# Order of a carry matmul and two scans within the step of a graph attention phase

## What is computed

```python
# layer 0, attention with 8 heads of 16 channels; src, tgt per edge
hi = x[src] @ w1
hj = x[tgt] @ w2
e = leaky_relu(hi + hj, 0.3) * a
logits = e.reshape(-1, 8, 16).sum(-1)
exp = jnp.exp(logits - segment_max(logits, tgt)[tgt])
attn = exp / segment_sum(exp, tgt)[tgt]
x = layernorm(x + segment_sum(hi.reshape(-1, 8, 16) * attn[:, :, None], tgt))
# layer 1, messages from nodes and edge attributes
ef = (relu(attr @ We1 + be1) @ We2 + be2) * sigmoid(t @ Wt + bt)
msg = relu(concat([x[src], ef]) @ Wn1 + bn1) @ Wn2 + bn2
x = layernorm(x + segment_sum(msg, dst) + x)
```

## Time and profile before

| | before |
|---|---|
| median of three runs | 2203.7 us |
| lowest and highest | 2195.6 and 2203.87 us |
| the profiled execution's own time | 2198.74 us |
| span of the profile | 2196.7 us |
| busy: PE, PE weight loads, DVE, ACT, POOL | 81%, 63%, 60%, 30%, 73% |
| mean granted PE clock | 0.906 of full speed |

### The profile page before, as it was taken

The page is one execution under the profiler, slowest core; times in us unless marked ns, Lnnn a source line. Parts: engine busy times, 40 slices in busy tenths (PEclk is TensorE's granted clock), DMA queues, the critical chain, the costliest instruction groups (busy, mean ns, idle before and its releaser), DMA issues.

```text
span 2196.7 us, 47111 instructions
## 1 busy us (share of the span) xinstructions
PE 1779.1 (81%) x12650; PEld 1394.1 (63%) x12721; DVE 1325.3 (60%) x3725; ACT 659.2 (30%) x1410; POOL 1602.8 (73%) x1701
## 2 busy tenths in 40 slices
PE   6787777777888888877869888888888788888877
PEld 5465555655666666655657667666666676667666
DVE  6555666666556666656645456666566566665655
ACT  6111111121111111111114434434444344444432
POOL 5777777777777777777527777777777777777775
PEclk9889998999888888899879999989999999999998
DMA  8722333333333333333255444444444444454441
GB/s 238 153 78 85 84 95 84 96 97 91 89 94 86 96 97 87 91 90 96 56 142 154 139 126 139 129 135 135 141 127 131 137 132 137 128 142 127 141 125 46
DMA packets 239385, 252.30 MB, mean 115 GB/s; under 512 B 141011, under 2 KB 187720, under 8 KB 239315
## 3 DMA queue, kind: packets, MB, share of 16 engines
q1 hardware_dynamic: 185036, 141.15, 21.8%
q0 software_dynamic: 54000, 110.28, 19.4%
q10 hardware_dynamic: 288, 0.13, 0.0%
HBM read 233.20 MB, written 13.22 MB: 112 GB/s over the span
## 4 chain that ended last, share of the span: by engine, by line
POOL 54%; issue 23%; PE 11%; DVE 5%; DMA 4%; DVEq 1%; POOLq 1%; ACT 1%; SPq 0%; ACTq 0%
POOL T L741 32%; POOL G L707 21%; PE ps L1854 2%; DMA G<-hi_rows,idx 2%; PE ps L1831 2%; PE ps L1826 2%; PE ps L1858 1%; PE ps L1787 1%; DVEq L1316 1%; DVE msg L1336 1%; ACT V L895 0%; DMA T<-y_rows,idx 0%; PE ps L2060 0%; DMA out<-T 0%; PE ps L2069 0%
## 5 line engine op out<-in xcount | busy, mean ns | idle before, releaser
L741 POOL DMA_INDIRECT T<-y_rows,idx x831 | 788.1, 948 | 307.3 <-issue 251.8
L707 POOL DMA_INDIRECT G<-hi_rows,idx x831 | 799.7, 962 | 263.2 <-issue 249.5
L2060 PE MATMUL ps<-G 128*128 128x64 f32 x1664 | 223.0, 279 | 125.9 <-DVE acc L1613 125.0
L999 ACT ACTIVATE G<-G 128x512 f32<-128x512 f32 x208 | 131.1, 630 | 577.6 <-DVE G L1619 577.6
L2060 PEld LDWEIGHTS ps<-G 128*128 128x128 f32 x1664 | 211.9, 199 | 137.8 <-issue 137.2
L1826 PE MATMUL ps<-ident,G 128*128 128x128 f32 x828 | 147.9, 307 | 180.0 <-issue 92.8
L1619 DVE TENSOR_TENSOR G<-ps,T 128x512 f32<-128x512 f32 x208 | 143.6, 690 | 218.8 <-DMA T<-y_rows,idx 207.4
L2069 PE MATMUL ps<-wN,G 128*128 128x128 f32 x1664 | 254.2, 300 | 23.2 <-DVE T L1578 23.2
L895 ACT ACTIVATE V<-ps 128x512 f32<-128x512 f32 x207 | 123.7, 598 | 468.3 <-PE ps L1831 462.6
L1307 DVE TENSOR_TENSOR V<-ps,V 128x512 f32<-128x512 f32 x207 | 141.8, 685 | 184.5 <-ACT V L895 181.9
L2081 PEld LDWEIGHTS ps<-msg,wE 128*128 128x128 f32 x832 | 170.2, 205 | 127.2 <-issue 112.3
(11 more groups left out here) (238 smaller groups left out, 2238.7 us busy)
## 6 DMA issues: line engine op xcount, KB each, us to landing
T<-in_edge_weight SPq DMA_DIRECT2D x103, 512.0 KB
Dbc<-block_destinations SPq DMA_DIRECT2D x69, 384.0 KB
T<-in_edge_attr SPq DMA_DIRECT2D x103, 256.0 KB
G<-hi_rows,idx POOLq DMA_INDIRECT x831
T<-y_rows,idx POOLq DMA_INDIRECT x831
link<-scan_destinations SPq DMA_DIRECT2D x280, 16.1 KB
hi_rows<-T SPq DMA_DIRECT2D x12, 256.0 KB, 4.6
mX<-in_x SPq DMA_DIRECT2D x15, 192.0 KB
```

Source lines behind the costliest of these rows:

```text
L707: pool.indirect_dma_start(out=G[:, s, t * C:(t + 1) * C], out_offset=None, in_=hi_d[:, :], in_offset=bass.IndirectOffsetOnAxis(ap=idx[:, s ...
L741: pool.indirect_dma_start(out=Yb[:, r, t * C:(t + 1) * C], out_offset=None, in_=y_d[:, :], in_offset=bass.IndirectOffsetOnAxis(ap=idx[:, r ...
L2060: ins = pe.matmul(sums_of(g4), hS[i][:, n * C:(n + 1) * C], ohB[i][:, n * W:(n + 1) * W], start=(n == 0), stop=(n == 3))
```

## The change

Two groups of statements change places with a neighbour, in the step of the first phase. On PE the downward carry, with its waits, stands ahead of aggregate(0); on DVE the second and third scan, with theirs, ahead of add(0).

```diff
@@ DVE, in step
                     leaky(2)
-                    add(0)
                     if b is not None:
 
                         dve.wait_ge(s_sh1, b + 1)
...
                         dve.tensor_tensor_scan(R3[0:BR, ::-1], link[:, bs, P:0:-1], R2[0:BR, ::-1], -1e30, ALU.add,
                                                ALU.max).then_inc(s_r3, 1)
+                    add(0)
                     nxt(2)
                     add(1)
@@ PE, in step
                     sums(2)
-                    aggregate(0)
                     if b is not None:
                         pe.wait_ge(s_r1, b + 1)
 
                         need(pe, s_msg, b)
                         pe.matmul(shp[0:BR, 0:1], down[0:BR, 0:BR], R1[0:BR, P - 1:P], start=True, stop=True).then_inc(s_sh1, 1)
+                    aggregate(0)
                     logits(f, s, 1)
```

## The result

| | before | after |
|---|---|---|
| median of 10 runs each | 2199.17 us (2194.6 to 2203.87) | 2205.24 us (2198.93 to 2209.6) |
| ratio after to before | | 1.0024, 95% interval 1.0013 to 1.0035 |
| profiled execution | 2198.74 us, span 2196.7 | 2205.65 us, span 2203.6 |

The change costs about 5 us, a quarter of a per cent.

A forecast was written before the change was run, and what follows sets the result against it. The prediction took POOL's issue of gathers to bound the first phase, with PE, DVE and ACT fitting beneath. Terms 0 + 0 + 4 + 0 + 0 = +4 us on 2198.7 gave 2203; it took 2204, range 2194 to 2216.

The forecast's parts named there:

- The wait on the first scan: First phase, PE: the carry matmul's new wait, 30 to 68 us in all, absorbed by PE's room; 0 on the path.
- Second and third scan earlier: First phase, DVE: scans start sooner but nothing takes their results sooner; gain on the path 0, at most 1.2 us.
- Collisions: First phase: delayed window one-hots lengthen POOL's gathers that start inside them; +4 us, bounds -9 to +21 us.
- The drain: Between the two phases' gathers: the carry matmul only changes places with aggregate(0); 0 us, 3 us allowed either way.
- Rival B: First phase: the new wait makes PE and DVE the bound, using up the message margin; about 2218 us, chance 0.05.
- the 2229 us: Whole kernel: total if the 30 us of new PE waits were paid in full; no chance of its own.
- Rival C: First phase: window one-hots settle just ahead of a gather in 30 steps now just clear; +21 us, 2220, chance 0.09.

The follow-up runs named there:

- iota_before: The kernel before, with the window one-hots' counting columns read from a PSUM bank instead of SBUF; ratio 0.9953 to before, 2192.34 us.
- iota_after: The changed kernel with the window one-hots' counting columns read from PSUM instead of SBUF; ratio 0.9955 to before, 2192.16 us.
- after_third: The changed kernel run again unaltered, on another chip beside 17 runs of the kernel before; ratio 1.0026 to before.
- dve_only: The kernel before with only DVE's half: second and third scan ahead of add(0), PE in the old order; ratio 1.0007 to before.
- pe_only: The kernel before with only PE's half: downward carry ahead of aggregate(0), DVE in the old order; ratio 0.9994 to before.

## Why the prediction was right, point by point

The forecast was no change within half a per cent, at 2204 us, with the cost, if any, in the gathers; measured 2205.24. That the time came within 1.3 us is partly luck. The forecast's change of +4 us started from a median of three runs, two of which were among the slowest of before (2203.7 us, over ten runs 2199.17), and from a profile at 2198.7; I took a value near the upper one. Against the ten runs the change is 6 us by the medians, 5 us by the ratio, and it is made up of a gather term twice as large as I took and a drain that was shorter in the profile.

1. **The wait on the first scan.** Expected in some 30 to 60 steps, about 1 us each, 30 to 68 us in all, paid by PE's room ahead of the third quad. It was 43 times, 31.4 us, at most 1.0 us, and the room shrank by 33.6 us (94.9 to 61.3). POOL waits for no message. iota_before against iota_after bounds the price on the path to about 3 us; that it is exactly 0 is not shown, see the drain.
2. **Second and third scan earlier.** Right: the second scan comes 1.4 us sooner relative to the third quad, the subtraction does not, as the fourth scan stands behind add(1). What the working missed is that the scans must move with the carry: alone, PE's half waits 18.9 us for the third scan.
3. **Collisions.** The right mechanism and an undersized term. I took +4 us, from late steps that spread over the 1.25 us between gathers. Measured are +8.2 us (after) and +6.6 us (after_third) in the gathers, +9 us in the hits. The step that was off is the halving, "about half of the steps are moved, so I take +4 us": the hits came to 18.5 us, the 19 us that the working had for all 67 one-hots at random places. More steps became late than I counted, 45 with the first scan over 1.0 us behind the third quad's start, where it was 34. That the full random value fits is no proof of random places. The delay varied less than I thought: in 36 of these 45 steps aggregate(0) came 2.14 to 2.4 us behind the third quad's start (1.14 before), and the one-hots crowd 0.2 to 0.45 us ahead of the gather (22 of 67; spread evenly it would be 13). So there were fewer hits than at random, 37 against 45, and dearer ones, 0.50 us against 0.42. Other instructions also changed their share, which the term left out: the fourth scan's fell from some 4 us to below 1, that of L1290 rose from 1.4 to 3.8 us in after and to 1.9 in after_third.
4. **The drain.** Given as 0, within 3 us either way; 52.0 and 55.3 us in the two profiles, against 54.2. So within it, but the working lacked a reason to move. I took from the last looped step of before that PE waits for its gathers at the end. With the new wait it need not: in three of the four profiles with PE's half, the last third quad starts 1.3 to 3.3 us after the gathers have ended, in the three others without added work 1.4 to 1.5 us before. Here PE's wait can reach the path once. The granted clock differs as well: in the 6 us from 1086 us on it was at 0.50 (1.2 GHz) in the kernel before, at 1.00 (2.4 GHz) in dve_only:

```profile
1086.00:1092.00 6.00, 5.78 (x35) 4.50 (x35) 1.50 (x6) 0.00 (x0) 0.00 (x0) 0.50 0.00 0
```

```profile
1086.00:1092.00 6.00, 6.00 (x59) 4.91 (x57) 3.87 (x11) 0.99 (x2) 0.76 (x1) 1.00 0.13 22
```

The gathers end 2.7 us apart in the two; counted from their end, the first 6 us of the drain are at 0.50 and 1.00 as well. In before PE had waited 1.97 us ahead of the last third quad, in dve_only 1.25 us. Why one fell to the lower clock and the other not stays open. It matters for the comparison: the two profiles without PE's half and without added work whose drain began at the full clock have drains of 49.6 (dve_only) and 49.0 us (iota_before), the four with PE's half 52.0 to 57.4 us. So PE's half may well cost about 3 us in the drain, hidden in the first pair of profiles by before's slow start of it. The times neither show nor exclude this.

Rival B did not come: the least margin of a message was 6.2 us in after and 5.7 in after_third, and POOL never waited for one. In pe_only it was 2.8 us, so the room was nearer its end there than the working supposed. One argument against B was wrong: slow steps did not become rarer with less idle time. In both kernels the transposes of 9 third quads took over 0.9 us, where 0.65 is the time at the full clock, and the granted clock of the stage was 0.88, where it was 0.90. They do stand behind long waits, as I wrote: 3.1 us on average in before, 1.1 us for the others.

The Trainium skill ("Perfetto Trace Analysis", section "Optimization Strategies") sets the goal of keeping the matmul engine as busy as possible. It names no price; the 2229 us in the prediction was my own reading of it, that each microsecond of idle PE is paid. iota_after, whose PE waits 32.8 us for the first scan and which is as fast as iota_before, shows that this reading does not hold where another engine sets the stage. Rival C came in part, with 14 more hits instead of 30. And the Trainium skill's page "SBUF — State Buffer", section "Who interferes with whom", was half right: two inputs in SBUF do contend with GpSimd, as before against iota_before shows, but its inference that a tensor_tensor leaves descriptor generation alone does not hold for these gathers.

## What to carry to other kernels

If one engine sets a stage and waits for nobody, ask of a reordering elsewhere not how long it makes the others wait but what it does to the durations of that engine's instructions: a group's sum against its count times its median shows at once what such collisions cost (14 us before, 23 us after the change). If a DVE instruction with two inputs in SBUF meets GpSimd's gathers, look at where it starts between them; moving one input of the window one-hots to PSUM took their collisions away, and the kernel was 0.45% faster, which is more than the order cost. And check whether waits that the room swallows are paid at the end of the stage, where the room ends.

## What was not expected of the hardware

- The place of one input decides whether the window one-hots hold up a gather: 0.96 us of one-hots from PSUM and SBUF, gathers of 0.95 us beside them; from SBUF twice, gathers of up to 1.80 us. It is not the only thing that counts: L1290, whose one large input is a bf16 tile in SBUF, holds up gathers as well, one of 1.12 us instead of 0.94.
- Where a gather starts within such an instruction, its end is set by that instruction and not by its own start: 0.81 to 0.84 us behind the end of the window one-hots in the 37 hits of the changed kernel.
